# Attention units' scores issued one place earlier, and masked earlier, in a one-core attention and mixture-of-experts kernel

## What is computed

```
q, k, v = silu(xn Wq), silu(xn Wk), silu(xn Wv)              # 16 heads of 32
per chunk of 128 tokens and per head, with decay ld:
  scores = (q k^T) * D                # D: lower triangle of exp(ld * (t - s))
  o      = scores v + (q S) * q_decay
  S      = exp(ld * 128) * S + (k * k_decay)^T v
o = rmsnorm_per_head(o * sigmoid(xn Wg1 Wg2)) * norm_w
attention = o Wo
experts: softmax(xn Wg), top 2 of 8, each expert keeps its first 1280 rows,
  relu(x_e w1_e) w2_e, weighted and added into the rows
```

## Time and profile before

| | |
|---|---|
| median of 3 runs | 1992.47 us (1992.23 to 1993.62) |
| profiled execution, its own time | 1994.35 us |
| span of the profiled execution, first to last instruction | 1992.6 us |
| TensorE busy | 1973.5 us, 99% of the span |
| VectorE, ScalarE, GpSimd busy | 904.4, 552.3, 731.9 us |
| mean granted TensorE clock | 0.998 |

### The profile page before, as it was taken

One profiled execution on the slowest core, in us unless ns is written; L12 is line 12 of the kernel. 1 busy time (PEld: TensorE's weight loads), 2 busy tenths in 40 slices (PEclk: granted clock), 3 DMA queues, 4 the chain that ended last, 5 costly groups with the idle time before them and its releaser, 6 DMA issues.

```text
span 1992.6 us, 29064 instructions
## 1 busy us (share of the span) xinstructions
PE 1973.5 (99%) x11672; PEld 1630.7 (82%) x11672; DVE 904.4 (45%) x1839; ACT 552.3 (28%) x994; POOL 731.9 (37%) x608
## 2 busy tenths in 40 slices
PE   8999999999999999999999999999999999999998
PEld 7888888888888888788788888888888888788887
DVE  8777676776843234235323422533253234224311
ACT  6322232323332223124112312421242123123211
POOL 4645454546342323314342431433142324323221
PEclk9999999999999999999999999999999999999999
DMA  6212122211442233315223431522162225224121
GB/s 199 73 65 87 44 66 73 79 65 50 137 141 35 56 78 114 49 48 143 59 59 77 122 44 53 132 62 43 46 161 37 45 56 150 38 58 103 41 33 21
DMA packets 85640, 151.53 MB, mean 76 GB/s; under 512 B 18432, under 2 KB 18432, under 8 KB 85488
## 3 DMA queue, kind: packets, MB, share of 16 engines
q1 hardware_dynamic: 61312, 105.64, 16.7%
q0 software_dynamic: 24176, 43.76, 12.9%
HBM read 109.82 MB, written 39.53 MB: 75 GB/s over the span
## 4 chain that ended last, share of the span: by engine, by line
PE 97%; DVE 2%; issue 0%; DMA 0%; POOL 0%; ACT 0%; SPq 0%; DVEq 0%; POOLq 0%
PE bank L1368 47%; PE bank L1672 35%; PE bank L1504 4%; PE bank L1422 2%; PE bank L1493 2%; PE bank L1375 1%; PE bank L1487 1%; PE bank L1728 1%; PE bank L1715 1%; PE bank L1457 1%; PE bank L1396 1%; PE bank L1467 1%; DVE stats L962 0%; DMA attn_raw<-in_L_attn_Wv 0%; DMA x_in<-in_L_attn_x 0%
## 5 line engine op out<-in xcount | busy, mean ns | idle before, releaser
L1289 DVE SCALAR_TENSOR_TENSOR h_lo<-bank,h_hi 128x512 fp32r<-128x512 f32 x254 | 175.3, 690 | 734.9 <-ACT h_hi L892 734.6
L670 POOL DMA_INDIRECT gathered<-xn_rows,gather_row x304 | 317.1, 1043 | 476.8 <-DVE x_blocks L1139 318.0
L1368 PE MATMUL bank<-xT_hi,w_hi 128*128 128x512 f32 x1024 | 399.7, 390 | 5.2 <-issue 5.2
L1368 PE MATMUL bank<-xT_hi,w_lo 128*128 128x512 f32 x1024 | 399.2, 390 | 2.2 <-issue 2.2
L1368 PE MATMUL bank<-xT_lo,w_hi 128*128 128x512 f32 x1024 | 399.0, 390 | 0.0
L1672 PE MATMUL bank<-w_hi,h_hi 128*128 128x512 f32 x1016 | 395.2, 389 | 0.0
L1672 PE MATMUL bank<-w_lo,h_hi 128*128 128x512 f32 x1016 | 395.2, 389 | 0.0
L1672 PE MATMUL bank<-w_hi,h_lo 128*128 128x512 f32 x1016 | 395.2, 389 | 0.0
L892 ACT ACTIVATE h_hi<-bank 128x512 fp32r<-128x512 f32 x254 | 151.7, 597 | 806.1 <-PE bank L1368 806.1
L691 POOL DMA_INDIRECT out_rows<-y,add_row x64 | 104.0, 1624 | 438.5 <-ACT y L885 422.5
L1368 PEld LDWEIGHTS bank<-xT_hi,w_hi 128*128 128x128 f32 x1024 | 192.6, 188 | 47.1 <-issue 7.1
(11 more groups left out here) (225 smaller groups left out, 2292.7 us busy)
## 6 DMA issues: line engine op xcount, KB each, us to landing
raw_weights<-in_L_ffn_w SPq DMA_DIRECT2D x256, 256.0 KB, 11.9
x_in<-in_L_attn_x SPq DMA_DIRECT2D x32, 256.0 KB, 4.3
xn_rows<-xn SPq DMA_DIRECT2D x32, 256.0 KB, 2.8
x_res<-in_L_attn_x SPq DMA_DIRECT2D x32, 256.0 KB, 5.0
out_rows<-y_attn SPq DMA_DIRECT2D x28, 256.0 KB, 2.0
gathered<-xn_rows,gather_row POOLq DMA_INDIRECT x304
out_rows<-y,add_row POOLq DMA_INDIRECT x88, 5.1
attn_raw<-in_L_attn_Wq SPq DMA_DIRECT2D x4, 256.0 KB, 5.2
```

The source lines that it names most:

```text
L670: pool.indirect_dma_start(xg[:, nth % 2, q * P:(q + 1) * P], None, xn_pieces, bass.IndirectOffsetOnAxis(ap=gather_row[:, col, q:q + 1], ax ...
L1289: v_.scalar_tensor_tensor(lo[:, 0:n * P], h_bank[f % 2][:, 0:n * P], 0.0, hi[:, 0:n * P].bitcast(F32), ALU.max, ALU.subtract).then_inc(S[" ...
L1368: last = mm(dest, at(left[l], t), at_r(right[r], t), start=(i == 0), stop=(i == n - 1))
```

## The change

`scored_ahead(u)` is true for the even units from 4 to 30: 14 units, seven with i = 0 (4, 8, ... 28) and seven with i = 2 (6, 10, ... 30).

On TensorE their `score` is no longer the first thing of their own turn. It is issued in the turn of the odd unit before, behind that unit's `attend` (and behind `update_states(u+1)` where that is done ahead), and so in front of the output products (i = 2 comes next) or of `turn_logits` and the value products (i = 0 comes next). On VectorE their `mask` moves from behind `states` of their own turn to behind `turn_gated` of the turn before, in front of the residuals and of the routing. No instruction is added or removed, and `score` keeps its own waits.

```diff
@@ build
+        def scored_ahead(u):
+
+            return GROUPS <= u < ATTN_UNITS - 1 and u % 2 == 0
@@ VectorE, loop over units
-                if u < ATTN_UNITS - 1:
+                if scored_ahead(u):
+                    states(u)
+                elif u < ATTN_UNITS - 1:
                     states(u)
                     mask(u, range(HPG))
@@
                 gate_output(u)
                 turn_gated(u)
+                if scored_ahead(u + 1):
+                    mask(u + 1, range(HPG))
@@ TensorE, loop over units
-                score(u)
+                if not scored_ahead(u):
+                    score(u)
                 if not updated_ahead(u):
                     update_states(u)
@@
                 attend(u)
                 if updated_ahead(u + 1):
                     update_states(u + 1)
+                if scored_ahead(u + 1):
+                    score(u + 1)
                 if i == 1 and g > 0:
```

## The result

| | before | changed |
|---|---|---|
| median of 6 runs each, same chip | 1992.35 us (1991.58 to 1993.62) | 2002.12 us (2000.26 to 2003.28) |
| profiled execution, its time | 1994.35 us | 2000.26 us |
| its span | 1992.6 us | 1998.5 us |

The ratio is 1.0045, 95% interval 1.0034 to 1.0056: slower by 6.8 to 11.2 us, 9.8 by the medians. The forecast was 2001.8 with 1998.7 to 2004.5.

The account below looks back on a forecast made before the run. TensorE, busy 99% of the span, was taken to bound the kernel. Seven times 0.64 us (output products) plus 0.69 us (value products) gave +9.3 us on 1992.47, so 2001.8 us, range 1998.7 to 2004.5.

Parts of the forecast that it names:

- TensorE's own row decides, and no wait could be removed: Whole kernel: TensorE is busy 99% of the span; its one attention-stage wait, 1.0 us in unit 0, precedes the change.
- Part A: Score ahead of the output products, seven times: k projection must wait for the fourth residual, +0.64 us each (0.47 to 0.77).
- The release: Output products: time from the end of the residual's bank read to TensorE's k projection, taken as 0.10 us.
- The restart: Output products: extra time of the k projection's matmuls after its wait, taken as 0.08 us, bounds 0 and 0.10.
- The unseen step from update to score: Ahead of the output products: state update to start of what follows, taken as 0.41 us as today, allowing -0.04 and +0.07.
- Part B: Score ahead of logits and value products, seven times: state update must wait for the fourth silu, +0.69 us each (0.64 to 0.73).
- V to update: Value products: start of the last value matmul to the state update, 1.13 us afterwards against 1.54 today.
- the block ahead: Between attend and the logits: the moved score adds 1.10 us, the step out of it included.
- The masks at nothing: VectorE: four moved mask instructions, 2.48 us, fourteen times, cost nothing; they end 0.2 us before the first residual is ready.
- Queues passed: Score's inputs and banks are ready at the new places; GpSimd's routing records for i = 2 go out some 6 us earlier.
- The rule that speaks for the change: Output products: three changes of the array's use become two, 0.20 us less, seven times, -1.4 us if nothing were awaited.
- The sum, +9.3: Whole kernel: 7 x (0.64 + 0.69) us added, bounds +7.8 to +10.5.

Follow-up runs that it names:

- e1: Against the kernel before, only the seven scores in front of the output products moved, with their masks: 2000.20 us, ratio 1.0021.
- e4: As e1, but the fourth output product goes into a free score bank: 1995.22 us, ratio 0.9992 to the kernel before; repeated, 1992.65 us, ratio 0.9994.
- e2: Against the kernel before, only the seven scores in front of the logits and value products moved, with their masks: 1999.08 us, ratio 1.0014.
- e3: The changed kernel with the masks back in their old place, all fourteen scores still ahead: 2003.49 us, ratio 1.0038 to the kernel before.
- the second comparison: The changed kernel, unaltered, measured again beside the kernel before: 2003.07 us, ratio 1.0047.
- e6: Changed kernel with fourth output and value products in a free score bank, state update behind the k projection: 1997.71 us, ratio 1.0012 to the kernel before.

## Why the prediction was right, point by point

- *TensorE's own row decides, and no wait could be removed:* borne out. Between two counts, all that differs on TensorE is the moved block with the steps around it, the two new waits and the slower restart; every other stretch agrees with the kernel before to 0.04 us.
- *Part A, +0.64 (0.47 to 0.77):* measured 0.71 by the steps above and 0.72 by the counts in e1. The release took 0.14 us, not 0.10. The restart took 0.11, not 0.08, and so more than the bound of 0.10: 0.08 in its first step, the rest in the ones behind it. The unseen step from update to score was as taken (303.18 to 303.59 in the trace, 0.41 as before). The cause is shown by e4: the same order without the bank's conflict gives -0.21.
- *Part B, +0.69 (0.64 to 0.73):* measured 0.49 in e2, outside its bounds. V to update was right (1.12 for 1.13). The term that was mis-sized is the block ahead: I took 1.10 plus today's steps around it, but the score in front of the four tiny transposes takes 1.01 to their start, and these are through after 0.29 instead of 0.34: 0.96 instead of 1.10. That I held the bounds by the release alone was the mistake: a new neighbour on both sides was taken as certain. The last 0.05 is the mean over the super-groups against the one read by steps (e2).
- *The masks at nothing:* shown by e3, 0.02 us per super-group. The 0.2 us of room in front of the first residual turned out as 0.45.
- *Queues passed:* the routing records of units with i = 2 went out 6.4 us after the output products' start instead of 13.1, without effect, as said.
- *The rule that speaks for the change:* fewer changes of the array's use are a gain, and e4 shows its size in the counts, 0.21 us where the steps gave 0.20. The Trainium skill (TensorEngine Tiling (Array Packing), Key Properties) says that a change of tiling mode drains the TensorE. The trace agrees that the order with one change fewer is shorter by 0.21 us; that a drain is the reason no run here shows. The wait and the restart took 0.93 (from -0.21 in e4 to +0.72 in e1), over four times as much.
- *The sum, +9.3:* the traces say +8.5, since A was 0.6 too low and B 1.4 too high over seven: two errors that partly cancel. That the median of the first comparison came out at 2002.12 beside 2001.8 is partly luck: its +9.8 and the +7.3 of the second comparison lie on either side of 8.5.

Not tried: a faster fourth residual or silu, for instance one cut in two, which should shorten each wait by what it saves.

## What to carry to other kernels

On an engine that never waits, look at what each block hides before you move it: compare the end of the eviction behind the last product with the start of the next writer or reader. That is the slack; what the block's length exceeds it by, plus the release and the restart, is what the move will cost (output products: 1.10 - 0.64 + 0.14 + 0.11 = 0.71). Where a block must move, give the product in front of it another bank, or put work that needs neither result into the gap. The bank was worth 0.93 us each time and the gate product 0.19, against 0.21 for the order itself. And when one wait is removed by delaying a step, look for who uses that step's result or its bank next.

## What the runs showed that I had not expected

- The step out of a block of 32-row matmuls depends on what follows: 1.10 us from the block's start to the next when a matmul of 512 or 32 columns follows, 1.01 us when a transpose of 16 columns does (337.53 to 338.54).
- Releases of TensorE took 0.14 us from the end of VectorE's residual (316.61 to 316.75) and 0.10 from the end of ScalarE's silu (350.64 to 350.74), where the mask of unit 0 released it after 0.05.
- VectorE took up a state update within 0.47 us of its start (98.06 to 98.53, changed kernel), but an idle VectorE only 1.92 us after it where the update stood between the k and the q projection (e6, 349.94 to 351.86). The cause is open.
- After a wait of 0.64 us the k projection's twelve matmuls took 2.85 us instead of 2.74.
- The distance between fixed points of the attention stage repeats to some hundredths of a microsecond (131.13 and 131.12 for the changed kernel, 128.30 twice for e4), while whole runs of one kernel scatter by several us.
